# Values in tiles of 64 rows, the gated layer's products on steps 0, 1, 2, 4 and 7 of ten, and the down product in two halves

## What is computed

```python
# attention: 16 heads of 16, causal
q, k, v = split(xn @ Wqkv.T);  dots = q k^T * 16 ** -0.5;  dots[future] = -inf
attn = softmax(dots);          out = merge(attn @ v) @ Wout.T + bout
# gated layer, with blocks of 16 numbers quantised to fp4 and back (q)
gate, up = q(xn) @ q(w_gate).T, q(xn) @ q(w_up).T       # 704 wide
h = silu(gate) * up;           y = q(h) @ q(w_down).T
```

## Time and profile before

| | |
|---|---|
| median of 3 runs | 2673.03 us (2672.72 to 2675.77) |
| the profiled execution, its own time | 2675.76 us |
| its span, first to last instruction | 2674.0 us |
| TensorE busy, share of the span | 2370.2 us, 89% |
| ScalarE busy | 2004.7 us, 75% |
| VectorE busy | 1876.6 us, 70% |
| GpSimd busy | 655.2 us, 25% |
| main phase: first exponential of the first batch | 989.2 us |
| first exponentials of batches 2, 3 and 4 | 1415.4, 1835.3, 2255.2 us |

### The profile page before, as it was taken

The page is one execution under the profiler, slowest core; times in us unless marked ns, Lnnn a source line. Parts: engine busy times, 40 slices in busy tenths (PEclk is TensorE's granted clock), DMA queues, the critical chain, the costliest instruction groups (busy, mean ns, idle before and its releaser), DMA issues.

```text
span 2674.0 us, 79088 instructions
## 1 busy us (share of the span) xinstructions
PE 2370.2 (89%) x28984; PEld 1202.2 (45%) x28984; DVE 1876.6 (70%) x5548; ACT 2004.7 (75%) x3470; POOL 655.2 (25%) x524
## 2 busy tenths in 40 slices
PE   1896999999999949999998999998999988999998
PEld 1784444444444423444444444444444444444445
DVE  6675999999999955665655656656566564666565
ACT  1343999999999948788866887885888885878875
POOL 3212333333333321222211221211222221212211
PEclk8897999999999979999999999999999999999999
DMA  2565555555555521101112011022011021110100
GB/s 64 181 228 126 72 73 73 72 73 73 72 73 72 73 57 29 27 17 26 28 51 51 17 24 30 16 54 60 14 27 29 14 56 47 26 29 16 26 17 33
DMA packets 94778, 143.50 MB, mean 54 GB/s; under 512 B 25264, under 2 KB 74160, under 8 KB 93872
## 3 DMA queue, kind: packets, MB, share of 16 engines
q1 hardware_dynamic: 73456, 113.77, 22.6%
q10 hardware_dynamic: 16576, 15.73, 1.8%
q0 software_dynamic: 4352, 8.92, 1.2%
HBM read 104.20 MB, written 34.14 MB: 52 GB/s over the span
## 4 chain that ended last, share of the span: by engine, by line
PE 39%; ACT 13%; issue 9%; DVE 1%; ACTq 1%; POOL 0%; DMA 0%; SPq 0%; POOLq 0%; DVEq 0%
ACT probs L1123 12%; PE O L994 11%; PE F L1014 10%; PE S L974 7%; PE F L1054 5%; PE S L1065 2%; PE F L1044 1%; PE S L980 1%; ACT ht_hi L1138 1%; ACTq L1110 1%; PE F L1007 1%; DMA y<-in_L_attn_x_dram 0%; ACTq L1118 0%; POOL h_norm L1186 0%; POOL h_fp L1192 0%
## 5 line engine op out<-in xcount | busy, mean ns | idle before, releaser
L1123 ACT ACTIVATE probs<-S 128x1024 f32<-128x1024 f32 (+3 forms) x1280 | 1059.5, 902 | 138.6 <-PE S L980 55.9
L775 ACT ACTIVATE m_excess<-m_DIFF 128x512 f32<-128x512 f32 (+7 forms) x1536 | 647.0, 472 | 85.8 <-PE m_DIFF L735 39.8
L793 DVE CUSTOM_DVE_ANT_0 m_excess<-m_S,m_excess 128x512 f32<-128x512 f32 (+7 forms) x1536 | 700.9, 538 | 11.7 <-PE m_S L735 9.4
L994 PE MATMUL O<-probs,v_sb 128*32 128x512 f32 (+3 forms) x5120 | 606.7, 546 | 4.0 <-POOL v_sb L1203 4.0
L974 PE MATMUL S<-q_st,k_st 64*32 64x512 f16 (+3 forms) x10240 | 433.4, 355 | 179.4 <-ACT probs L1123 133.6
L733 PE MATMUL m_S<-m_k,m_q 128*128 128x512 f16 (+7 forms) x1536 | 483.1, 325 | 26.7 <-DVE m_row_max L793 17.3
L733 PE MATMUL m_DIFF<-m_k,m_q_diff 128*128 128x512 f16 (+7 forms) x1536 | 477.9, 319 | 26.4 <-DMA m_q_diff<-s_q 26.1
L974 PEld LDWEIGHTS S<-q_st,k_st 64*32 64x32 f16 x10240 | 129.0, 90 | 608.6 <-ACT probs L1123 500.6
L677 POOL TENSOR_TENSOR m_q_diff<-m_zero,m_q 48x4096 f16<-48x4096 f16 x32 | 224.4, 7011 | 429.1 <-DMA m_q<-s_q 418.4
L733 PEld LDWEIGHTS m_S<-m_k,m_q 128*128 128x128 f16 x1536 | 148.3, 97 | 275.9 <-DVE m_row_max L793 195.0
L1300 DVE TENSOR_SCALAR tanh<-tanh 128x352 int32<-128x352 int32 x128 | 49.4, 386 | 266.1 <-ACT decay L1133 266.1
(11 more groups left out here) (176 smaller groups left out, 4061.5 us busy)
## 6 DMA issues: line engine op xcount, KB each, us to landing
m_q<-s_q SPq DMA_DIRECT2D x96, 128.0 KB, 3.7
m_k<-s_k SPq DMA_DIRECT2D x96, 128.0 KB, 6.8
m_q_diff<-s_q SPq DMA_DIRECT2D x96, 128.0 KB, 8.1
k_st<-s_k SPq DMA_DIRECT2D x96, 128.0 KB, 4.3
q_st<-s_q SPq DMA_DIRECT2D x384, 32.0 KB
m_k<-s_k SPq DMA_DIRECT2D x96, 124.0 KB, 5.3
a_x<-in_L_attn_x_dram POOLq DMA_DIRECT2D x16, 512.0 KB, 4.6
s_q<-a_part SPq DMA_DIRECT2D x32, 256.0 KB, 2.5
```

The costliest lines, as they stand in the source:

```text
L775: act.activation(excess[u % MAX_EXCESS][:, 0:keys // 2], DIFF[u % MAX_BUFS][:, 0:keys // 2], ACT.Relu) \
L793: dve.tensor_tensor_reduce(larger, S[u % MAX_BUFS][:, 0:keys // 2], larger, 1.0, -3e38, ALU.add, ALU.max, column).then_inc(reduced[u % MAX ...
L994: ins = pe.matmul(o[s * SLOT:(s + 1) * SLOT, st.skip:QC], v_sb[st.hg % 2][:, st.j, s * SLOT:(s + 1) * SLOT], probs[s // 2][st.n % 2][:, s ...
L1123: act.activation(probs[half][st.n % 2][:, :, 0:st.width], S[half][:, :, 0:st.width], ACT.Exp, scale=scale).then_inc(exped[half], 1)
```

## The change

- `values`: each of the four heads' matmuls is split into two, rows 0 to 63 into bank O[0] and rows 64 to 127 into bank O[1]. Both banks serve every chunk, so `values` of a new chunk waits for the turning of the chunk just before, where it waited for the one before that.
- `normalise` turns both banks, adds the two (new, `o_sum`), and goes on from the sum. It comes first in a step's VectorE work, where it came last.
- x_turn goes from k = 0 to k = 2, gate+up from 3 and 6 to 4 and 7 (tile 0 keeps 5 and 8), h_turn from k = 8 of the tile after to k = 0 of the tile after that (for tile 14: k = 9 of tile 15), down from k = 0 to two halves of 9 matmuls at k = 1 and k = 2. The work of the other engines that belongs to them moves with it; in VectorE, gate_chunk comes before the other work of the step.
- `PROBS = 2` names the number of `probs` buffers, which stays 2.

```diff
-TURN_AT, PAIR_AT = 0, {3: 0, 6: 1}
-FIRST_TURN_AT, FIRST_PAIR_AT = 2, {5: 0, 8: 1}
-H_TURN_AT = 8
+X_TURN_AT, PAIR_AT, FIRST_PAIR_AT = 2, {4: 0, 7: 1}, {5: 0, 8: 1}
+H_TURN_AT, DOWN_AT = 0, (1, 2)
+LAST_H_TURN_AT = 9
...
+def h_turned_at(n, k, tiles):
+
+    if k == H_TURN_AT and n >= 2:
+        return n - 2
+    return tiles - 2 if k == LAST_H_TURN_AT and n == tiles - 1 else None
...
-                o = O[st.chunk % 2]
                 if st.c == 0 and st.first:
                     pe.wait_ge(v_ready, b * NHG + st.hg + 1 + PRIMED)
                 if st.first:
-                    pe.wait_ge(o_free[st.chunk % 2], b * (chunks // 2) + st.chunk // 2 + PRIMED)
+                    pe.wait_ge(o_free[(st.chunk + 1) % 2], b * (chunks // 2) + (st.chunk + 1) // 2 + PRIMED)
                 for s in range(HG):
-                    ins = pe.matmul(o[s * SLOT:(s + 1) * SLOT, st.skip:QC], v_sb[st.hg % 2][:, st.j, s * SLOT:(s + 1) * SLOT],
-                                    probs[s // 2][st.n % 2][:, s % 2, 0:st.width], start=st.first, stop=st.last)
+                    for e in range(2):
+                        rows = rows_of(e)
+                        ins = pe.matmul(O[e][s * SLOT:(s + 1) * SLOT, st.skip:QC],
+                                        v_sb[st.hg % 2][rows, st.j, s * SLOT:(s + 1) * SLOT],
+                                        probs[s // 2][st.n % PROBS][rows, s % 2, 0:st.width], start=st.first, stop=st.last)
                 ins.then_inc(pv_done, 1)
...
-            def down(b, n):
-                pe.wait_ge(ht_lo_done, b * 2 * tiles + 2 * (n + 1) + PRIMED)
-                if n == tiles - 2:
-                    pe.wait_ge(gated_done, b * 2 * tiles + 2 * tiles + PRIMED)
-                terms = [(h, w, m) for m in range(ITILES) for h, w in
-                         ((ht_hi, wts["down_hi"]), (ht_hi, wts["down_lo"]), (ht_lo, wts["down_hi"]))]
-                for k, (h, w, m) in enumerate(terms):
-                    ins = pe.matmul(F[1][:, 0:D], h[:, m * P:(m + 1) * P], w[:, m, :],
-                                    start=k == 0, stop=k == len(terms) - 1)
-                ins.then_inc(down_ps, 1)
+            def down(b, n, part):
+                if part == 0:
+                    pe.wait_ge(ht_lo_done, b * 2 * tiles + 2 * (n + 1) + PRIMED)
+                for m in range(part * ITILES // 2, (part + 1) * ITILES // 2):
+                    for h, w in ((ht_hi, wts["down_hi"]), (ht_hi, wts["down_lo"]), (ht_lo, wts["down_hi"])):
+                        ins = pe.matmul(F[1][:, 0:D], h[:, m * P:(m + 1) * P], w[:, m, :],
+                                        start=m == 0 and w is wts["down_hi"] and h is ht_hi,
+                                        stop=m == ITILES - 1 and h is ht_lo)
+                if part:
+                    ins.then_inc(down_ps, 1)
...
-                    if k == 0 and n >= 2:
-                        down(b, n - 2)
-                    if k == turned_at(n):
+                    if k in DOWN_AT and n >= 2:
+                        down(b, n - 2, DOWN_AT.index(k))
+                    if k == X_TURN_AT:
                         x_turn(b, n)
                     if ch is not None:
                         gate(b, n, ch)
                         up(b, n, ch)
-                    if k == H_TURN_AT and n >= 1:
+                    turned = h_turned_at(n, k, tiles)
+                    if turned is not None:
                         for part in range(2):
-                            h_turn(b, n - 1, part)
-                down(b, tiles - 2)
+                            h_turn(b, turned, part)
+                for part in range(2):
+                    down(b, tiles - 2, part)
...
-                    elif k == 5 and n + 1 < tiles:
+                    elif k == 6 and n + 1 < tiles:
                         x_rescale(b, n + 1)
-                    elif k == 8:
+                    elif k == 9:
...
-                    dve.transpose(o_turned[:, :], O[chunk % 2][:, :]).then_inc(o_free[chunk % 2], 1)
+                    ch.tick(dve.transpose(o_turned[0][:, :], O[0][:, :]))
+                    dve.transpose(o_turned[1][:, :], O[1][:, :]).then_inc(o_free[chunk % 2], 1)
+                    ch.sync()
                     dve.wait_ge(o_free[chunk % 2], b * (chunks // 2) + chunk // 2 + 1 + PRIMED)
-                    turned = o_turned[:, :].rearrange("p (a s) -> p a s", s=SLOT)
-                    ch.tick(dve.reciprocal(o_rsum[:, :], turned[:, :, DH]))
+                    low, high = (t[:, :].rearrange("p (a s) -> p a s", s=SLOT)[:, :, 0:DH + 1] for t in o_turned)
+                    ch.tick(dve.tensor_tensor(o_sum[:, :, :], low, high, ALU.add))
+                    ch.sync()
+                    ch.tick(dve.reciprocal(o_rsum[:, :], o_sum[:, :, DH]))
                     ch.sync()
...
-                    if k == 0:
+                    if st.n and steps[st.n - 1].last:
+                        normalise(steps[st.n - 1].chunk)
+                    turned = h_turned_at(n, k, tiles)
+                    if turned is not None:
+                        for part in range(2):
+                            h_low(turned, part)
+                    if chunk_at(n, k) is not None:
+                        gate_chunk(n, chunk_at(n, k))
+                    if k == 1 and n + 1 < tiles:
+                        x_scales(n + 1)
+                    elif k == DOWN_AT[-1]:
                         if n >= 2:
                             add_down(n - 2)
                         x_low(n)
-                    elif k == 1 and n + 1 < tiles:
-                        x_scales(n + 1)
-                    elif k == 2 and n >= 1:
+                    elif k == 3 and n >= 1:
                         h_round_(n - 1)
-                    elif k == 3:
-                        gate_chunk(n, 0)
-                    elif k == 4 and n + 1 < tiles:
+                    elif k == 5 and n + 1 < tiles:
                         x_round_(n + 1)
-                    elif k == 6:
-                        gate_chunk(n, 1)
-                    elif k == 7:
+                    elif k == 8:
                         h_scales(n)
-                    elif k == H_TURN_AT and n >= 1:
-                        for part in range(2):
-                            h_low(n - 1, part)
-                    if st.n and steps[st.n - 1].last:
-                        normalise(steps[st.n - 1].chunk)
```

More of the change, by code:

```diff
@@ L823, in attention_steps @@
     return steps
-TURN_AT, PAIR_AT = 0, {3: 0, 6: 1}
-FIRST_TURN_AT, FIRST_PAIR_AT = 2, {5: 0, 8: 1}
-H_TURN_AT = 8
+X_TURN_AT, PAIR_AT, FIRST_PAIR_AT = 2, {4: 0, 7: 1}, {5: 0, 8: 1}
+H_TURN_AT, DOWN_AT = 0, (1, 2)
+LAST_H_TURN_AT = 9
 def quarters():
     return [slice(a * SLOT, (a + 1) * SLOT) for a in range(P // SLOT)]
-def turned_at(n):
-    return TURN_AT if n else FIRST_TURN_AT
 def chunk_at(n, k):
     return (PAIR_AT if n else FIRST_PAIR_AT).get(k)
+def h_turned_at(n, k, tiles):
+    if k == H_TURN_AT and n >= 2:
+        return n - 2
+    return tiles - 2 if k == LAST_H_TURN_AT and n == tiles - 1 else None
 def main_phase(nc, once, loop_sems, wts, ident, exp_scale, x_rows, bout, out_rows, dram):
@@ L876, in main_phase @@
         v_in, v_sb = sb("v_in", [P, NKB, D]), two("v_sb", [P, NKB, HG * SLOT])
-        probs = [two(f"probs{h}_", [P, 2, QC]) for h in range(2)]
-        o_turned = sb("o_turned", [P, QC])
+        probs = [[sb(f"probs{h}_{n}", [P, 2, QC]) for n in range(PROBS)] for h in range(2)]
+        o_turned = two("o_turned", [P, QC])
+        o_sum = sb("o_sum", [P, QC // SLOT, DH + 1])
         o_rsum = sb("o_rsum", [P, QC // SLOT])
@@ L882, in main_phase @@
         S = [ps(f"S{h}", [P, 2, QC]) for h in range(2)]
-        O = [ps(f"O{c}", [P, QC]) for c in range(2)]
+        O = [ps(f"O{e}", [P, QC]) for e in range(2)]
         F = [ps(f"F{f}", [P, 512]) for f in range(2)]
@@ L1100, in _ @@
                     elif m == FLUSH_DOWN:
-                        down(b, tiles - 1)
+                        for part in range(2):
+                            down(b, tiles - 1, part)
                     project(b, m)
@@ L1118, in exps @@
                 act.wait_ge(scored[half], b * nsteps + st.n + 1 + PRIMED)
-                if st.n >= 2:
-                    act.wait_ge(pv_done, b * nsteps + st.n - 1 + PRIMED)
+                if st.n >= PROBS:
+                    act.wait_ge(pv_done, b * nsteps + st.n - PROBS + 1 + PRIMED)
                 else:
                     act.wait_ge(pv_done, b * nsteps + PRIMED)
-                act.activation(probs[half][st.n % 2][:, :, 0:st.width], S[half][:, :, 0:st.width], ACT.Exp,
+                act.activation(probs[half][st.n % PROBS][:, :, 0:st.width], S[half][:, :, 0:st.width], ACT.Exp,
                                scale=scale).then_inc(exped[half], 1)
@@ L1152, in _ @@
                         gate_parts(b, n, ch)
-                    if k == H_TURN_AT and n >= 1:
+                    turned = h_turned_at(n, k, tiles)
+                    if turned is not None:
```

(7 more changed lines are left out.)

## The result

The changed kernel takes 2657.39 us (median of 5 runs, 2652.71 to 2661.22) against 2673.76 for the kernel before in runs beside it: a ratio of 0.9936, 95% interval 0.9925 to 0.9947. That is 16.4 us faster, where 28 were forecast; 2645.5 was the forecast time. The profiled execution took 2657.39 us with a span of 2655.6.

What follows compares the result with a forecast made beforehand. TensorE and ScalarE take turns, neither full. Per batch -11.9 - 2.3 + 4.9 + 1.8 = -7.5 us, -30 in four; 2.6 given back for matmuls makes -27.5, so a median of 2645.5 us; range 2622 to 2686.

Steps and rivals of the forecast that it cites:

- Change of shape, 0.13: On TensorE, each change between tile shapes costs 0.13 to 0.14 us; with one shape, scores to values falls from 0.34.
- Twice the matmuls cost 0.01: On TensorE, splitting values into twice the matmuls adds 0.01 us for each values group, 2.6 us over some 256 groups.
- The new places: Moved TensorE work uses idle time of three steps instead of two; with the shape, 1.19 us saved in a tile.
- the ten plain tiles: Tiles 2, 3, 5, 6, 7, 9, 10, 11, 13 and 14: -1.19 us each, -11.9 in a batch.
- Tiles 4, 8 and 12, +4.9: Down waits for ht_lo behind VectorE's scales and normalise, late by 2.0, 2.7 and 2.0 us; less savings, +4.9 a batch.
- One pair of banks at k = 4, covered by gate+up: At a chunk's end at k = 4, the 2.12 us of gate+up cover the wait of values for turning both banks.
- a sign of being wrong: The profile after would show the forecast wrong if values waited for O at k = 2 and 4 as well.
- One pair of banks at k = 2, "nearly" covered: At a chunk's end at k = 2, half of down with x_turn nearly covers the turning of 0.71 + 0.60 us.
- Tile 1 was to gain 1.7: Tile 1 loses h_turn (1.14 us) and has the two gate+up and x_turn: about -1.7 us in a batch.
- The tail, +1.8: The 12.38 us chain from the last gate+up to tile 15's h_turn moves from step 6 to 7: +1.8 us a batch.
- Tile 0, -0.6: Tile 0 has two gate+up, 2 x 0.13, and a narrow x_turn step with some 0.3 less: -0.6 us.
- The rival of a VectorE that is no obstacle: Scales come earlier at tiles 4, 8, 12 and ht_lo is not waited for: 34 us more gained, 2611; chance 0.12.

Runs made afterwards that it cites:

- e1: The kernel before, with values from rows 0 to 63 only, in the scores' 64x32 shape, and the reciprocal reading a tile of ones: 2683.86 us, ratio 1.0032.
- e9: e5 with the last tile a step earlier, but values, two O banks by turns and single turning as in the kernel before: 2628.3 us, ratio 0.9829.
- e4: The changed kernel with tile 0's gate and up at steps 4 and 7 instead of 5 and 8: 2645.4 us, ratio 0.9891.
- e3: The changed kernel, but VectorE makes ht_lo between turning the two O banks and the sum: 2627.43 us, ratio 0.9823.
- e5: The changed kernel with the edits of e3 and e4 together: 2619.38 us, ratio 0.9793.
- e6: The changed kernel's values and normalise with the places of the kernel before: 2725.97 us, ratio 1.0191, one run of 6629 us left out of the ratio.

## Why the prediction came out as it did

The direction and the range held, and so did the shape's cost and the places' gain; what the one pair of banks costs was sized too low, and the gain was forecast 1.7 times too large. By its steps, for the second batch, where 419.9 us became 415.8 (the main phase's first exponentials stand at 1408.3 and 1824.1 after):

- *Change of shape, 0.13.* Right: 0.34 to 0.22, and e1 and e9 show that it is the shape and not the type. The rule of the Trainium skill (TensorEngine Tiling, section "Key Properties"), a drain at a change of tiling mode, agrees with the traces; it gives no price.
- *Twice the matmuls cost 0.01.* Right, and if anything too high: 1.04 against 1.07, and 0.86 to the next scores. By the floor of about 25 ns in the Trainium skill (TensorE: Matmul & The Clock Gate, section "Wait — 56ns, not 53.3ns?") values would have taken an estimated 0.1 longer; the trace disagrees for matmuls that go to separate tiles.
- *The new places.* Right in the sum: the ten plain tiles gave 12.9 us a batch for 11.9 forecast, and in tile 3 steps 0, 1 and 2 take 2.84, 2.69 and 2.89 for 2.83, 2.67 and 2.90. Not every tile follows it (in tile 2 they take 2.90, 2.64 and 2.60, and step 5 has the wait at k = 4).
- *Tiles 4, 8 and 12, +4.9.* The queue was right: down starts 5.5 us after h_turn in tile 8, behind what was written down. TensorE itself comes later than the sum had it, so it is idle for 1.2, 1.95 and 1.2 where 2.0, 2.7 and 2.0 stood; just before, it had waited 0.37 for the turning. In tiles 4 and 12 the tile's sum held (+1.3 each for +1.4). **In tile 8 it failed**: +4.6 for +2.1, since the clock falls in the wait and down and the scores behind it run at half speed. An estimate from tile 4: its 24.9 us and the 0.7 us of longer wait would make 25.6, near the 25.7 of the forecast, and the 2.6 above that are the fall's. The forecast had priced a wait at its length only.
- *One pair of banks at k = 4, covered by gate+up.* **This failed**, and the forecast had named it as a sign of being wrong. The 2.12 of gate+up were counted from the end of values, but VectorE was in the rounding of h: 0.72 us of wait and 0.41 of step at seven borders, 2.9 us a batch. It did not show in the tile's sums, since it lies in tiles that gained more elsewhere than forecast; that the ten tiles' sum held is in part luck.
- *One pair of banks at k = 2, "nearly" covered.* **This failed too.** Tile 1 was to gain 1.7 and lost 0.8. I had priced the turning from when values end, and not looked at what VectorE does then: it was still in the scales of tile 2, themselves slowed by GpSimd. The wait of 1.24 and the fall behind it are 2.5 us a batch, 10 of the 12 us that e4 gets back.
- *The tail, +1.8.* Tile 15 with the tail takes 1.7 more in the first batch and 2.4 in the second, where the clock falls in the wait of down of tile 14 for `ht_lo`. The chain from the last gate+up to h_turn is 12.39 us (1376.72 to 1389.11), as forecast.
- *Tile 0, -0.6.* -1.5, of which the clock has a part: 0.92 for 0.86.

Together: -7.5 forecast, before the 0.65 given back for the matmuls; -4.1 measured. Of the difference of 3.4, tile 1 is 2.5, tile 8 2.4 and the tail 0.6, and tile 0 (0.9), the ten plain tiles (1.0) and tiles 4 and 12 (0.3) went the other way. Without these gains, that nobody had forecast, the time would have been further off. The rival of a VectorE that is no obstacle was false for this kernel, but e3 and e4, which make it true in part, show what it is worth: 30 and 12 us, and 38 together (e5), for the 34 of the rival.

Not settled: why the clock falls in some waits and not in others. In the change it falls in all four waits of tile 8 (1.95 us) and of tile 1 (1.24), in one of the eight of tiles 4 and 12 (1.2), and in three of the four at the down of tile 14 (1.9); with the order of e3 the same wait of 1.24 in tile 1 has a fall in two batches of four. So the length of the wait alone does not decide it. Nor is it settled why values of half the rows (e1) lose it without a wait. A run with other work put into the wait of tile 8 was not made, since all eight banks are taken.

## What to carry to other kernels

When a double buffer is given up to gain a faster shape, the wait that comes with it must be priced from the reader's whole queue, at the place where it falls, and not from the length of the read; put the freeing operation first in that queue and split what follows from it. "First in its step" is not first in the queue: at the borders at k = 4 work of the step before still stood ahead of it, and that wait is in the best of these kernels too. A pause of TensorE of a microsecond or two in a thin stretch can cost twice its length, because the work behind it may run at half the clock: look for PEclk below 1.00 tile by tile, and count it as part of the wait. And undo the parts one at a time: places alone were 10 us better than the whole change, while the parts together, once their queue was put right, were 21 us better still than the places with the same order.

## What the runs showed of the hardware

- fp32 matmuls in eight tiles of 64 x 32 run as fast as in four of 128 x 32: 1.04 us for 512 columns against 1.07, with 16 rows in the trace for 8.
- Between scores and values of one shape nothing is lost, fp16 to fp32 and back (0.22 and 0.86 from start to start).
- TensorE's granted clock fell to 0.50 after stretches in which it had run 1.31 of 3.40 us (tile 1) and 0.82 of 3.40 (e6), and was low for 3.4 to 6.8 us. With half of the array's rows idle in values (e1), the clock of a batch was 0.94 instead of 0.99; what causes it was not shown.
- Two small VectorE operations of 0.17 us took 0.78 and 0.65 when they began during an operation of GpSimd (1.40 and 0.72 long), and ended 0.03 after it, in all four batches.
